# A prologue in another order: second keys projected early into other PSUM banks, loads from two queues, two roundings moved

## The chip, the cores and the metric

One core of a Trainium2 chip runs one transformer block, everything in one launch. The metric is the device time in microseconds. The kernel is written engine by engine: TensorE (PE), VectorE (DVE), ScalarE (ACT), GpSimd (POOL) and SyncE (SP) each have one list of instructions, and semaphores tie the lists together. An engine never passes over an instruction that waits, so the order of each list matters.

## The reference

The input `x` is 4 batches of 256 rows of 256 numbers, and `ctx_2048` has the same shape. Cut to what matters:

```
h  = layernorm(x);  hq = fp8_round(h / in_scale) * in_scale      # for q, qx, k, v: four roundings
q, qx = hq @ wq.T, hq @ wqx.T          # 16 heads of 128 each
k, v  = hq @ wk.T, hq @ wv.T           # 8 groups of 128
kx,vx = split(ctx @ w_kv_x.T)          # 8 groups, from the context, not rounded
each of q, qx, k, kx: layernorm over its 128 numbers
self  = softmax(q k') v;  cross = softmax(qx kx') vx             # grouped-query attention
x1 = x + tanh(g_xattn) * fp8_round([self, cross] * smooth) @ wproj.T
x2 = x1 + tanh(g_ffn) * (routed top-6 of 64 experts + shared expert)(layernorm(x1))
```

The change touches only the start: the first layernorm, its roundings, and the first keys and values.

## The kernel before, in words

**The loop.** After a prologue, all engines run the same written-out loop `for i in range(NSUB + MAXLAG)`, 34 rounds. A round starts one sub-block `s0 = sub(i)` (two of the 16 heads, for both kinds of attention, for one batch) and carries on the two before it, `s1` and `s2`. `n = a // 2` names a unit (one batch and one pair of groups), `t` one half (128 rows) of its sequence. `kv_at(i)` says which half of which unit's keys and values a round projects: round 0 does (0, 1), round 1 does (1, 0), round 2 does (1, 1), and so on. Half (0, 0) is done in the prologue. After the loop come the router and the experts.

**The prologue, per engine.** SP loads x for batches 0 and 1, seven of fifteen small vectors (`load_vectors`, L388), x for batches 2 and 3, the first key and value weights (`load_kv(0, 0)`, L409), the context (L436), the cross-attention weights (`load_kv(0, 1)`) and the first query weights. ACT issues the other eight vectors and then eight scalars `scal` (L700), before its first computation. All vectors land in rows of one tile, `vec_rows`, which PE turns once all fifteen are there (L1431); DVE takes them over (`vectors`, L971).

For each batch b of x: DVE takes statistics (`ln_stats`), POOL raises to the power -1/2 (`ln_rstd`), DVE normalises (`ln_norm`), PE turns the result (`transpose_h`), ACT scales it (`ln_out(b)`, L651) and writes four scaled copies (`quant_y(b)`, L660), and then DVE rounds them to fp8 by adding and taking away a magic number: `quant_exponents(b)` and `quant_round(b)`. The last subtraction is POOL's for batches 0 and 1 (`quant_sub`, L509) and DVE's for 2 and 3 (`quant_less`, L1001). Only two batches have buffers (`q_y[b % 2]`, `q_mg[b % 2]`), and these lie over tiles that the loop needs: `q_mg[0]` over `qk_f`, so the first turned keys (`evac_Tk(0, 0)`, L764) wait for three roundings (`xq_ready` 3). Before, the fourth batch's rounding stands on DVE in round 0, ahead of the sums of the first queries' squares.

PE also turns the context (`transpose_ctx`, through the two banks of `pT_ps`, which the loop later uses for turned probabilities) and the weights (`fill_kv`, `fill_wq`, through the two banks `aux_ps`); for each, ACT takes the high part (`ctx_hi`, `kv_hi`, `wq_hi`) and DVE the rest (`ctx_lo`, `kv_lo`, `wq_lo`), each matrix being kept as a high and a low float.

**Keys.** `project_kv(n, t)` (L1449) writes both kinds of keys and values of one half into the two banks of `proj_ps`. ACT squares the keys (`squares_kv`, L728) and copies the values out (`evac_v`, L742); DVE sums (`sums`, L1079); POOL makes the reciprocal root (`rstd_of`, L519); DVE scales (`scaled_kv`, L1085, signals `qk_normed`). The queries' `project_q`, `squares_q`, `rstd_q` and `scaled_q` do the same, in the same two banks `proj_ps`, so each projection waits for the scaling of the one before it (`wait(pe, qk_normed, seq)`). The scaled tiles are turned by PE (`fill_Tk`, `fill_Tq`), taken out by ACT (`evac_Tk`, `k_hi`, `evac_Tq`, `q_hi`) and finished by DVE (`qk_lo`, L1108); then `scores` can start (L1520).

Of the kernel before, what the change touches and what calls it, by code (L numbers as in the profile page):

```python
# [5 lines left out]
def flamingo_kernel(nc: bass.Bass, t: dict, out: bass.AP):  # L6
# [38 lines left out]
    with ctx:  # L45
# [346 lines left out]

        @block.sync
        def _(sp):
# [11 lines left out]
            def load_rows(dst, name, row, n, done):  # L406
                sp.dma_start(dst, t[name][row:row + n * D, :].rearrange("(r p) h -> p r h", p=P)).then_inc(done, 16)

            def load_kv(j, x):  # L409

                a, b = ((("L0_xattn_wk", 0), ("L0_xattn_wv", 0)), (("L0_xattn_w_kv_x", 0), ("L0_xattn_w_kv_x", G * D)))[x]
                load_rows(w_raw[:, 4 * x:4 * x + 2, :], a[0], a[1] + 2 * j * D, 2, w_loaded[x])
                load_rows(w_raw[:, 4 * x + 2:4 * x + 4, :], b[0], b[1] + 2 * j * D, 2, w_loaded[x])

            def load_wq(g, dst, done):

                load_rows(dst[:, 0:2, :], "L0_xattn_wq", g * HPG * D, 2, done)
                load_rows(dst[:, 2:4, :], "L0_xattn_wqx", g * HPG * D, 2, done)
# [22 lines left out]
            load_kv(1, 0)  # L441
# [5 lines left out]
            for j in range(G // 2):  # L447
                if j > 0:
# [4 lines left out]
                    if j + 1 < G // 2:  # L453
                        sp.wait_ge(aux_filled, Fill("WQ", 1, 2 * j).filled)
                        load_kv(j + 1, 0)
                sp.wait_ge(aux_filled, Fill("WQ", 1, 2 * j + 1).filled)
                if j + 1 < G // 2:
                    load_kv(j + 1, 1)
# [33 lines left out]
        def _(pool):  # L492
# [26 lines left out]
            def rstd_of(seq, last, w):  # L519

                at = slice(0, 4) if w == 4 else slice(4, 12)
# [9 lines left out]
            def rstd_kv(n, t):  # L531

                rstd_of(kv_seq(n, t), kv_seq(n - 1 + t, 1 - t) if (n, t) != (0, 0) else -1, 4)

            def rstd_q(s):
                rstd_of(q_seq(s.a), q_seq(s.a - 1) if s.a else -1, 8)
# [26 lines left out]
            rstd_kv(0, 0)  # L563
            quant_sub(1)
            for i in range(NSUB + MAXLAG):
# [5 lines left out]
                if kv:  # L571
                    rstd_kv(*kv)
# [70 lines left out]
        def _(act):  # L643
# [53 lines left out]
            act.wait_ge(rows_clear, 1)  # L697
            load_vectors(act, VECTORS[7:])
# [6 lines left out]
            ln_out(1)  # L705
            quant_y(1)
# [7 lines left out]
            ln_out(2)  # L714
            quant_y(2)
# [12 lines left out]
            def squares_kv(n, t):  # L728
# [3 lines left out]
                nc.scalar.activation(sq[:, 0:4 * D].rearrange("p (a b) -> p a b", a=2), proj_ps[:, :, 0:2 * D],  # L732
# [9 lines left out]
            def evac_v(n, t):  # L742
# [3 lines left out]
                if at >= VRING:  # L746
                    act.wait_ge(aux_filled, Fill("Vx", 2 * ((at - VRING) // 2) + 1).filled)
                nc.scalar.activation(v_sb[:, at % VRING, :, :, :].rearrange("p y g d -> p y (g d)"),
                                     proj_ps[:, :, 2 * D:4 * D], ACT.Copy).then_inc(v_ready, 1)
# [83 lines left out]
            evac_v(0, 0)  # L833
            wq_hi(0, 0)
            wq_hi(1, 0)
            ln_out(3)
            for i in range(NSUB + MAXLAG):
# [4 lines left out]
                if kv:  # L842
                    squares_kv(*kv)
# [3 lines left out]
                if kv:  # L847
                    evac_v(*kv)
                if i == 0:
                    quant_y(3)  # L850
# [88 lines left out]
        def _(dve):  # L939
# [139 lines left out]
            def sums(seq, w):  # L1079

                dve.wait_ge(sq_ready, seq + 1)
                nc.vector.tensor_reduce(ss[:, w - 4:2 * w - 4], sq[:, 0:w * D].rearrange("p (a d) -> p a d", d=D), AX.X,  # L1082
                                        ALU.add).then_inc(ss_ready, 1)

            def scaled_kv(n, t):  # L1085
# [3 lines left out]
                if n > 0:  # L1089
# [3 lines left out]
                    proj_ps[:, :, 0:2 * D].rearrange("p x (a d) -> p x a d", d=D),  # L1093
                    rstd[:, 0:4].rearrange("p (x a) -> p x a", x=2).unsqueeze(3).to_broadcast([P, 2, 2, D]),
# [124 lines left out]
            quant_exponents(2)  # L1219
            scaled_kv(0, 0)  # L1220
            wq_lo(0, 0)
            wq_lo(1, 0)
            quant_round(2)
            for i in range(NSUB + MAXLAG):
                s0, s1, s2, kv = sub(i), sub(i - 1), sub(i - 2), kv_at(i)
                if kv:
                    sums(kv_seq(*kv), 4)
# [9 lines left out]
                if kv:  # L1237
# [143 lines left out]
        def _(pe):  # L1381
# [67 lines left out]
            def project_kv(n, t):  # L1449
# [20 lines left out]
                for i, (c, a, w) in enumerate(terms):  # L1470
                    ins = nc.tensor.matmul(proj_ps[:, 1, :], ctxT[:, a, c, tok], wkvT[:, w, c, 1, :],  # L1471
# [3 lines left out]
            def project_q(s):  # L1475
# [4 lines left out]
                wait(pe, qk_normed, seq)  # L1480
                wait(pe, v_ready, min(s.a + 2, 2 * NU))
# [332 lines left out]
```

## Time and profile before

| | us |
|---|---|
| median of 3 runs (lowest to highest) | 804.56 (802.93 to 805.38) |
| the profiled execution, its own time | 801.96 |
| its span, first to last instruction | 800.1 |

| engine | busy us | share of the span |
|---|---|---|
| PE | 718.0 | 90% |
| DVE | 604.1 | 76% |
| ACT | 466.1 | 58% |
| POOL | 447.4 | 56% |

The busy time says how long an engine worked, the span how long the whole took. The mean granted clock of PE was 0.977 of full speed. The profile has several views: the page with its slices, the timeline of an engine (each row: start, duration, what, and in brackets the idle time before it and who ended it), the chain of waits, the windows. The part that the change touches lies in the first 60 us.

### The profile page before, as it was taken

How to read it: one execution, taken by the hardware profiler on the slowest of the kernel's cores; microseconds unless marked ns; L12 is line 12 of the kernel's file. 1: busy time of each engine (PE TensorE's matmuls, PEld its weight loads, DVE VectorE, ACT ScalarE, POOL GpSimd, SP SyncE). 2: the span in 40 equal slices, each digit the busy share in tenths (PEclk: the TensorE clock that was granted, in tenths of full speed). 3: DMA queues.
4: the chain of work that ended last, by engine and by line, in shares of the span. 5: the costliest groups of instructions: out<-in, count | busy, mean ns of one | idle time of the engine just before them, and what ended most of it. 6: DMA issues, size and time to landing. Idle time of an engine off the chain costs nothing.

```text
span 800.1 us, 15318 instructions
## 1 busy us (share of the span) xinstructions
PE 718.0 (90%) x4857; PEld 582.8 (73%) x4857; DVE 604.1 (76%) x1286; ACT 466.1 (58%) x1179; POOL 447.4 (56%) x586
## 2 busy tenths in 40 slices
PE   3648899899999989999998999998978778999996
PEld 3546787788788778878877887887756556777775
DVE  6867888788888878888887888889888673444444
ACT  5646767677676767767666776866754322222221
POOL 3415777566777756677775667776766223222220
PEclk9979999999999999999999999999999897999999
DMA  5310100100010010001001010000010104666661
GB/s 185 112 53 1 53 3 1 54 28 28 0 45 10 1 54 27 27 1 40 16 1 54 1 34 2 27 1 2 1 42 19 67 9 132 195 190 189 192 186 54
DMA packets 44478, 42.74 MB, mean 53 GB/s; under 512 B 3717, under 2 KB 43386, under 8 KB 44410
## 3 DMA queue, kind: packets, MB, share of 16 engines
q1 hardware_dynamic: 41706, 36.61, 14.9%
q0 software_dynamic: 1536, 5.28, 2.5%
q8 instruction: 35, 0.57, 0.3%
q14 instruction: 33, 0.27, 0.1%
q10 hardware_dynamic: 1168, 0.01, 0.1%
HBM read 39.52 MB, written 2.37 MB: 52 GB/s over the span
## 4 chain that ended last, share of the span: by engine, by line
PE 63%; DVE 18%; ACT 6%; issue 6%; POOL 4%; DMA 1%; SPq 1%; POOLq 0%; DVEq 0%; ACTq 0%
PE out_ps L1748 9%; PE s_ps L1530 6%; PE proj_ps L1486 6%; PE proj_ps L1471 6%; PE pT_ps L1539 5%; DVE q_tok L1102 5%; PE aux_ps L1549 4%; PE aux_ps L1500 4%; PE aux_ps L1563 4%; PE proj_ps L1462 4%; PE work_ps L1740 3%; POOL rstd L528 3%; DVE pT_sb L1127 3%; DVE ss L1082 3%; PE work_ps L1762 2%
## 5 line engine op out<-in xcount | busy, mean ns | idle before, releaser
L543 POOL TENSOR_SCALAR p_sb<-p_sb,psum_row 128x256 f32<-128x256 f32 x256 | 125.0, 503 | 67.9 <-DVE psum_row L1121 66.6
L797 ACT ACTIVATE p_sb<-s_ps,negmax 128x256 f32<-128x256 f32 x256 | 118.3, 473 | 64.1 <-DVE negmax L1116 63.0
L1549 PE MATMUL aux_ps<-pT_sb,v_sb 128*128 128x512 f32 x256 | 120.7, 594 | 4.0 <-DVE pT_sb L1127 4.0
L1530 PE MATMUL s_ps<-kT,qT 128*128 128x256 f32 x768 | 112.3, 289 | 8.2 <-DVE qT L1112 4.6
L1127 DVE COPY pT_sb<-pT_ps 128x512 f32<-128x512 f32 x128 | 87.7, 686 | 41.3 <-PE pT_ps L1539 40.8
L550 POOL TENSOR_TENSOR y_bf<-y_bf,mg_bf 128x512 bf16<-128x512 bf16 x64 | 85.8, 1341 | 58.5 <-DVE mg_bf L1139 58.5
L1530 PEld LDWEIGHTS s_ps<-kT,qT 128*128 128x128 f32 x768 | 97.6, 190 | 18.3 <-issue 18.3
L1116 DVE TENSOR_REDUCE negmax<-s_ps 128x2 f32<-128x512 f32 x128 | 86.5, 683 | 5.9 <-PE s_ps L1530 5.6
L528 POOL TENSOR_TENSOR rstd<-var,minus_half 128x8 f32<-128x8 f32 (+1 forms) x64 | 85.7, 1339 | 5.3
L553 POOL TENSOR_TENSOR catq<-y_bf,mg_bf 128x512 fp32r<-128x512 bf16 x64 | 79.5, 1243 | 5.0
L1748 PE MATMUL out_ps<-eo,onehot 128*128 128x256 f32 x512 | 74.2, 297 | 0.6 <-ACT eo L909 0.6
L1563 PE MATMUL aux_ps<-wpT,catq 128*128 128x256 f32 x512 | 69.2, 288 | 5.9 <-DVE wkvT L1030 4.8
L1748 PEld LDWEIGHTS out_ps<-eo,onehot 128*128 128x128 f32 x512 | 66.2, 193 | 9.9 <-issue 8.6
L1539 PE MATMUL pT_ps<-ident,p_sb 128*128 128x128 f32 x512 | 72.0, 273 | 0.9 <-POOL p_sb L543 0.7
L633 POOL DMA_INDIRECT gx<-rows_dram,idx_cur x32 | 33.0, 1031 | 69.0 <-DVE w_slot L1331 59.8
L1486 PE MATMUL proj_ps<-wqT,xq 128*128 128x256 f32 x512 | 67.0, 284 | 4.0 <-DVE k_tok L1091 4.0
L1549 PEld LDWEIGHTS aux_ps<-pT_sb,v_sb 128*128 128x128 f32 x256 | 44.1, 190 | 35.4 <-issue 35.4
L1563 PEld LDWEIGHTS aux_ps<-wpT,catq 128*128 128x128 f32 x512 | 63.2, 191 | 6.8 <-DVE wkvT L1030 5.5
L1486 PEld LDWEIGHTS proj_ps<-wqT,xq 128*128 128x128 f32 x512 | 63.6, 191 | 4.3 <-issue 4.3
L1539 PEld LDWEIGHTS pT_ps<-ident,p_sb 128*128 128x128 f32 x512 | 59.4, 140 | 6.6 <-POOL p_sb L543 2.5
L760 ACT ACTIVATE qk_f<-aux_ps,vec 128x512 f32<-128x512 f32 x64 | 49.8, 778 | 23.6 <-PE aux_ps L1500 21.0
L909 ACT ACTIVATE eo<-work_ps,w_slot 128x256 fp32r<-128x256 f32 x32 | 15.2, 474 | 82.7 <-PE work_ps L1762 82.7
(181 smaller groups left out, 1399.2 us busy)
## 6 DMA issues: line engine op xcount, KB each, us to landing
w_up_a<-in_L_ffn_gate_up_proj SPq DMA_DIRECT2D x16, 384.0 KB, 3.5
w_up_b<-in_L_ffn_gate_up_proj SPq DMA_DIRECT2D x16, 384.0 KB, 3.6
wp_raw<-in_L_xattn_wproj SPq DMA_DIRECT2D x16, 256.0 KB, 2.9
w_down_a<-in_L_ffn_down_proj SPq DMA_DIRECT2D x16, 192.0 KB, 3.5
w_down_b<-in_L_ffn_down_proj SPq DMA_DIRECT2D x16, 192.0 KB, 3.6
w_raw<-in_L_xattn_w_kv_x SPq DMA_DIRECT2D x8, 256.0 KB, 3.3
w_raw<-in_L_xattn_wq SPq DMA_DIRECT2D x7, 256.0 KB, 2.7
w_raw<-in_L_xattn_wqx SPq DMA_DIRECT2D x7, 256.0 KB, 2.9
```

The lines of the kernel that those rows point to most:

```text
L528: nc.gpsimd.tensor_tensor(rstd[:, at], var8[:, at], minus_half[:, 0:w], ALU.pow).then_inc(rstd_ready, 1)
L543: ins = nc.gpsimd.tensor_scalar(p_sb[:, r, st, :], p_sb[:, r, st, :], rsum[:, r, st:st + 1], 1.0, ALU.mult, ALU.mult)
L550: nc.gpsimd.tensor_tensor(yc_bf[:, ty, :], yc_bf[:, ty, :], mg_bf[:, ty, :], ALU.add).then_inc(catq_ready, 1)
L797: ins = nc.scalar.activation(p_sb[:, r, st, :], s_ps[:, r % 2, st, :], ACT.Exp, bias=negmax[:, r, st:st + 1], accum_out=psum_row[:, r, st: ...
L1116: nc.vector.tensor_reduce(negmax[:, r, :], s_ps[:, r % 2, :, :], AX.X, ALU.max, negate=True).then_inc(max_ready, 1)
L1127: nc.vector.tensor_copy(pT_sb[:, r // 2, r % 2, :, :], pT_ps[:, r % 2, :, :]).then_inc(pT_ready, 1)
L1486: ins = nc.tensor.matmul(proj_ps[:, t, x * 256:(x + 1) * 256], xq[:, s.b, 3 * x, c, t * P:(t + 1) * P], wqT[:, s.gi, part, c, x * 256:(x + ...
L1530: ins = nc.tensor.matmul(s_ps[:, k % 2, st, :], qT[:, a, ty, h, st * P:(st + 1) * P], kT[:, b, ty, s.gi, :], start=(i == 0), stop=(i == 2))
L1539: ins = nc.tensor.transpose(pT_ps[:, r % 2, tt, st * P:(st + 1) * P], p_sb[:, r, st, tt * P:(tt + 1) * P], ident[:, :])
L1549: ins = nc.tensor.matmul(aux_ps[:, f.bank, :], v_sb[:, (2 * s.n + tt) % VRING, ty, s.gi, :], pT_sb[:, ty, :, tt, :], start=(tt == 0), stop ...
L1563: ins = nc.tensor.matmul(aux_ps[:, f.bank, tt * H:(tt + 1) * H], catq[:, s.gi, blk, tt * P:(tt + 1) * P], wpT[:, s.gi, part, blk, :], star ...
L1748: ins = nc.tensor.matmul(out_ps[:, n, :], onehot[:, u % 2, n * P:(n + 1) * P], eo[:, part, :], start=False, stop=False, skip_group_check=True)
```

## The change

All of `x` is issued first on SP, then all fifteen vectors, then the first query weights. ACT issues the first key and value weights, the context and the cross-attention weights, then the scalars. The second half of the first unit's keys, (0, 1), leaves round 0: it is projected straight behind (0, 0), into the banks of `pT_ps`, and has its own four places in `ss`, `var8` and `rstd` (`kv_stats`). ACT does `ln_out(1)`, `quant_y(1)` behind the weights and context instead of before them, and batch 2 behind both halves of the keys and the first query weights. The fourth batch's rounding moves on DVE behind `qk_lo` of the first turned keys, and on ACT behind `k_hi`.

```diff
+        def kv_ps(n, t):
+            return pT_ps[:, :, :, :].rearrange("p a b c -> p a (b c)") if (n, t) == (0, 1) else proj_ps[:, :, :]
+
+        def kv_stats(n, t):
+            return slice(4, 8) if (n, t) == (0, 1) else slice(0, 4)
...
 @block.sync
-            load_x(0)
-            load_x(1)
+            for b in range(NB):
+                load_x(b)
             sp.wait_ge(rows_clear, 1)
-            load_vectors(sp, VECTORS[:7])
-            load_x(2)
-            load_x(3)
+            load_vectors(sp, VECTORS)
...
-            load_kv(0, 0)
-            sp.dma_start(ctx_raw, t["ctx_2048"].rearrange("b (n p) h -> p (b n) h", p=P)).then_inc(ctx_loaded, 16)
-            load_kv(0, 1)
             load_wq(0, wq0_raw, wq0_loaded)
...
 @block.gpsimd
-                rstd_of(kv_seq(n, t), kv_seq(n - 1 + t, 1 - t) if (n, t) != (0, 0) else -1, 4)
+                rstd_of(kv_seq(n, t), kv_seq(n - 1 + t, 1 - t) if n > 0 else -1, kv_stats(n, t), 4)
...
             rstd_kv(0, 0)
+            rstd_kv(0, 1)
             quant_sub(1)
...
 @block.scalar
-            act.wait_ge(rows_clear, 1)
-            load_vectors(act, VECTORS[7:])
+            load_kv(act, 0, 0)
+            act.dma_start(ctx_raw, t["ctx_2048"].rearrange("b (n p) h -> p (b n) h", p=P)).then_inc(ctx_loaded, 16)
+            load_kv(act, 0, 1)
...
             ln_out(0)
             quant_y(0)
-            ln_out(1)
-            quant_y(1)
             ctx_hi(0)
             ctx_hi(1)
...
             ctx_hi(2)
             ctx_hi(3)
-            ln_out(2)
-            quant_y(2)
+            ln_out(1)
+            quant_y(1)
...
             squares_kv(0, 0)
             evac_v(0, 0)
+            squares_kv(0, 1)
+            evac_v(0, 1)
             wq_hi(0, 0)
             wq_hi(1, 0)
+            ln_out(2)
+            quant_y(2)
             ln_out(3)
             for i in range(NSUB + MAXLAG):
...
-                if kv:
+                if kv and i > 0:
                     squares_kv(*kv)
...
-                if i == 0:
-                    quant_y(3)
...
                     k_hi(s0.n, 0)
+                if i == 0:
+                    quant_y(3)
...
 @block.vector
             quant_exponents(1)
             quant_round(1)
             sums(0, 4)
-            quant_exponents(2)
+            sums(kv_seq(0, 1), 4)
             scaled_kv(0, 0)
+            scaled_kv(0, 1)
             wq_lo(0, 0)
             wq_lo(1, 0)
+            quant_exponents(2)
             quant_round(2)
...
-                if i == 0:
-                    quant_exponents(3)
-                    quant_round(3)
-                    quant_less(3)
                 if s0:
                     sums(q_seq(s0.a), 8)
...
                     qk_lo(s0.n, "TKs")
+                if i == 0:
+                    quant_exponents(3)
+                    quant_round(3)
+                    quant_less(3)
...
 @block.tensor
-                wait(pe, qk_normed, seq)
-                wait(pe, v_ready, 2 * n + t)
+                if (n, t) == (0, 1):
+                    pe.wait_ge(ctx_ready, 4)
+                else:
+                    wait(pe, qk_normed, seq)
+                    wait(pe, v_ready, 2 * n + t)
...
-                wait(pe, qk_normed, seq)
-                wait(pe, v_ready, min(s.a + 2, 2 * NU))
+                wait(pe, qk_normed, seq if s.a else 1)
+                wait(pe, v_ready, min(s.a + 2, 2 * NU) if s.a else 1)
...
             project_kv(0, 0)
+            project_kv(0, 1)
             fill_wq(0, 0)
             fill_wq(1, 0)
```

PE's own list of the prologue is otherwise as it was: `transpose_h(3)`, the last thing ahead of `project_kv(0, 0)`, waits for `ln_out(1)` (`yT_ready` 2).

## Rows read from the trace of the kernel before

**Rows 1.** The page: busy time by engine.

```profile
PE 718.0 (90%) x4857; PEld 582.8 (73%) x4857; DVE 604.1 (76%) x1286; ACT 466.1 (58%) x1179; POOL 447.4 (56%) x586
```

**Rows 2.** The chain of waits, 0 to 60 us: start, duration, what.

```profile
6.11 8.63 DMA p_sb<-in_ctx
...
25.53 3.31 ACT wp_raw L666 x8
...
47.64 2.29 DVE xq L1005
...
51.54 1.65 POOL rstd L528
```

**Rows 3.** Timeline of the queue on SP.

```profile
0.75 0.97 SPq L396 DMA_DIRECT2D x_sb<-in_x  x2
1.77 0.36 SPq L391 DMA_DIRECT2D sq<-in_L_xattn_ln_w  x1
...
3.73 0.32 SPq L391 DMA_DIRECT2D sq<-in_L_xattn_proj_smooth  x1
...
6.69 3.07 SPq L407 DMA_DIRECT2D w_raw<-in_L_xattn_w_kv_x  x2
```

**Rows 4.** Timeline of ACT.

```profile
7.22 0.58 ACTq L700 DMA_DIRECT2D scal<-in_g_ffn  x1
7.83 1.28 ACT L702 ACT_TABLE_LOAD   x1 [7.83 <-issue]
...
9.23 1.00 ACT L656 ACTIVATE acc<-s_ps,vec 128x256 f32<-128x256 f32 x2
...
23.51 1.08 ACT L647 ACTIVATE ctxT<-pT_ps 128x512 fp32r<-128x512 f32 x2
...
28.74 0.58 ACT L732 ACTIVATE sq<-proj_ps 128x512 f32<-128x512 f32 x1
...
31.12 1.03 ACT L656 ACTIVATE acc<-s_ps,vec 128x256 f32<-128x256 f32 x2
```

**Rows 5.** Timeline of DVE.

```profile
7.24 0.21 DVE L974 COPY vec<-proj_ps 128x52 f32<-128x52 f32 x1 [0.74 <-PE proj_ps L1431]
...
13.42 0.62 DVE L983 TENSOR_SCALAR wscale<-vec,scal 128x2 f32<-128x2 f32 x4 [0.43 <-DMA scal<-in_g_ffn]
...
19.86 0.88 DVE L1027 SCALAR_TENSOR_TENSOR wkvT<-aux_ps,wscale,wkvT 128x256 fp32r<-128x256 f32 x2 [0.84 <-ACT wkvT L680]
...
34.50 2.33 DVE L998 TENSOR_SCALAR qk_f<-qk_f 128x2048 bf16<-128x2048 bf16 x1
...
44.21 0.68 DVE L992 TENSOR_SCALAR v_sb<-v_sb 128x2048 bf16<-128x2048 bf16 x1
...
49.85 1.21 DVE L1082 TENSOR_REDUCE ss<-sq 128x8 f32<-128x1024 f32 x1
53.21 1.23 DVE L1102 TENSOR_TENSOR q_tok<-proj_ps,rstd 128x1024 f32<-128x1024 f32 x1 [2.15 <-POOL rstd L528]
...
57.18 0.69 DVE L1112 TENSOR_TENSOR qT<-qk_f,qT 128x512 fp32r<-128x512 f32 x1 [2.15 <-ACT qT L782]
```

**Rows 6.** Timeline of PE.

```profile
6.75 0.45 PE L1431 MATMUL proj_ps<-ident,sq 128*128 128x128 f32 x1 [6.75 <-DMA sq<-in_L_xattn_proj_smooth]
...
17.40 1.06 PE L1407 MATMUL aux_ps<-center,w_raw 128*128 128x128 f32 x4
...
22.08 0.68 PE L1407 MATMUL aux_ps<-center,w_raw 128*128 128x128 f32 x4 [0.30 <-DVE wkvT L1027]
...
33.12 1.61 PE L1462 MATMUL proj_ps<-wkvT,xq 128*128 128x256 f32 x8 [4.08 <-DVE k_tok L1091]
...
59.52 1.67 PE L1530 MATMUL s_ps<-kT,qT 128*128 128x256 f32 x12
```

**Rows 7.** Timeline of POOL.

```profile
32.21 4.07 POOL L512 TENSOR_TENSOR xq<-v_sb,y_bf 128x2048 fp32r<-128x2048 bf16 x1
```

**Rows 8.** DMA issues of 0 to 40 us: KB each, median us from issue to landing.

```profile
scal<-in_g_ffn ACTq DMA_DIRECT2D x1, 0.5 KB, 6.2
```

More of the change, by code:

```diff
@@ L391, in load_vectors, with load_rows, load_kv @@
                 eng.dma_start(vec_rows[row:row + n, :], t[name].rearrange("(r p) -> r p", p=P)).then_inc(vec_loaded, 16)
+        def load_rows(eng, dst, name, row, n, done):
+            eng.dma_start(dst, t[name][row:row + n * D, :].rearrange("(r p) h -> p r h", p=P)).then_inc(done, 16)
+        def load_kv(eng, j, x):
+            a, b = ((("L0_xattn_wk", 0), ("L0_xattn_wv", 0)), (("L0_xattn_w_kv_x", 0), ("L0_xattn_w_kv_x", G * D)))[x]
+            load_rows(eng, w_raw[:, 4 * x:4 * x + 2, :], a[0], a[1] + 2 * j * D, 2, w_loaded[x])
+            load_rows(eng, w_raw[:, 4 * x + 2:4 * x + 4, :], b[0], b[1] + 2 * j * D, 2, w_loaded[x])
         @block.sync
@@ L397, in load_x @@
                              ).then_inc(x_loaded[b], 16)
-            load_x(0)
-            load_x(1)
+            for b in range(NB):
+                load_x(b)
             sp.wait_ge(rows_clear, 1)
-            load_vectors(sp, VECTORS[:7])
-            load_x(2)
-            load_x(3)
[L406 to L413, printed above, removed]
+            load_vectors(sp, VECTORS)
             def load_wq(g, dst, done):
-                load_rows(dst[:, 0:2, :], "L0_xattn_wq", g * HPG * D, 2, done)
-                load_rows(dst[:, 2:4, :], "L0_xattn_wqx", g * HPG * D, 2, done)
+                load_rows(sp, dst[:, 0:2, :], "L0_xattn_wq", g * HPG * D, 2, done)
+                load_rows(sp, dst[:, 2:4, :], "L0_xattn_wqx", g * HPG * D, 2, done)
             def load_wp(g):
@@ L440, in _ @@
             load_wq(1, w_raw[:, 4:8, :], w_loaded[1])
-            load_kv(1, 0)
+            load_kv(sp, 1, 0)
             sp.wait_ge(aux_filled, Fill("WQ", 1, 0).filled)
@@ L454, in _ @@
                         sp.wait_ge(aux_filled, Fill("WQ", 1, 2 * j).filled)
-                        load_kv(j + 1, 0)
+                        load_kv(sp, j + 1, 0)
                 sp.wait_ge(aux_filled, Fill("WQ", 1, 2 * j + 1).filled)
                 if j + 1 < G // 2:
-                    load_kv(j + 1, 1)
+                    load_kv(sp, j + 1, 1)
                 else:
@@ L517, in _, with rstd_of @@
             quant_sub(0)
-            def rstd_of(seq, last, w):
-                at = slice(0, 4) if w == 4 else slice(4, 12)
+            def rstd_of(seq, last, at, w):
                 pool.wait_ge(ss_ready, seq + 1)
@@ L731, in squares_kv @@
                 wait(act, ss_ready, seq)
-                nc.scalar.activation(sq[:, 0:4 * D].rearrange("p (a b) -> p a b", a=2), proj_ps[:, :, 0:2 * D],
+                nc.scalar.activation(sq[:, 0:4 * D].rearrange("p (a b) -> p a b", a=2), kv_ps(n, t)[:, :, 0:2 * D],
                                      ACT.Square).then_inc(sq_ready, 1)
@@ L748, in evac_v @@
                 nc.scalar.activation(v_sb[:, at % VRING, :, :, :].rearrange("p y g d -> p y (g d)"),
-                                     proj_ps[:, :, 2 * D:4 * D], ACT.Copy).then_inc(v_ready, 1)
+                                     kv_ps(n, t)[:, :, 2 * D:4 * D], ACT.Copy).then_inc(v_ready, 1)
             def evac_Tq(s, ty):
@@ L841, in _ @@
                     k_hi(s1.n, 1)
-                if kv:
+                if kv and i > 0:
                     squares_kv(*kv)
@@ L846, in _ @@
                 weights_hi(i, 1)
-                if kv:
+                if kv and i > 0:
                     evac_v(*kv)
-                if i == 0:
-                    quant_y(3)
                 if i == 2:
@@ L1225, in _ @@
                 s0, s1, s2, kv = sub(i), sub(i - 1), sub(i - 2), kv_at(i)
-                if kv:
+                if kv and i > 0:
                     sums(kv_seq(*kv), 4)
@@ L1236, in _ @@
                     recip(s1, 0)
-                if kv:
+                if kv and i > 0:
                     scaled_kv(*kv)
@@ L1461, in project_kv @@
                         for part in range(2):
-                            nc.tensor.matmul(proj_ps[:, 0, ty * 256:(ty + 1) * 256],
+                            nc.tensor.matmul(kv_ps(n, t)[:, 0, ty * 256:(ty + 1) * 256],
                                              xq[:, b, 1 + ty, c, t * P:(t + 1) * P],
@@ L1470, in project_kv @@
                 for i, (c, a, w) in enumerate(terms):
-                    ins = nc.tensor.matmul(proj_ps[:, 1, :], ctxT[:, a, c, tok], wkvT[:, w, c, 1, :],
+                    ins = nc.tensor.matmul(kv_ps(n, t)[:, 1, :], ctxT[:, a, c, tok], wkvT[:, w, c, 1, :],
                                            start=(i == 0), stop=(i == len(terms) - 1))
@@ L1617, in _ @@
                 s0, s1, s2, kv = sub(i), sub(i - 1), sub(i - 2), kv_at(i)
-                if kv:
+                if kv and i > 0:
                     project_kv(*kv)
```

9 lines of the change are left out of this document (5 added, 4 removed).

## The prediction

> **What bounds the kernel now, and how I read it.** The page first: PE is busy for 90% of the span [rows 1], and nearly all of that is the loop and the experts, which the change leaves alone. So the question is by how much the start of the steady loop moves, and that is settled in the first 60 us, where PE mostly waits. The chain of waits there [rows 2] shows what ends last: the landing of the context at 14.74 us (6.11 + 8.63), then ACT's scaled copies of batch 2 (3.31), the rounding of batch 3 on DVE (the last of it 2.29), POOL's root (1.65). It passes through four engines, so I read their timelines next, each for two marks. Mark S is where ACT starts `ctx_hi(2)`, 23.51 us: by then the first weights are converted. Mark F is the first score matmul, 59.52 us, after which both kernels run the same instructions [rows 4, 6]. Before, F - S = 36.0 us. The change moves S by its loads and its early order, and F - S by its late order. I work out both.
>
> **Loads.** The SP queue issued two of x in 0.97 us (the next row starts 1.02 after it) and seven vectors in 2.28 us, 1.77 to 4.05, so 0.33 each; ACT issued eight more of the same kind beside them [rows 3]. Now SP issues four of x and all fifteen vectors: 0.75 + 2.04 + 15 x 0.33 = 7.7 us for the end of the last, at the 0.30 of the shortest 7.3. From the start of the last issue of before (3.73) to PE's first instruction (6.75) were 3.02 us [rows 3, 6]. Thus the vectors are all there at about 7.2 + 3.0 = 10.2 us, against 6.75: 3.5 us later. Bounds: 9.2 if the last one, a single row now and not the 16 KB of `proj_smooth`, lands 1 us faster after its issue (my guess; the least that its place allows is 6.75 plus eight issues of 0.30 more, the same 9.2); 12.0 if it is slowed as `scal` was (6.2 us from issue to landing, beside 1 KB packets of the big loads [rows 8]), in part. I take 10.3, near to the row of the same kind of load.
>
> The context is issued at about 2.0 us instead of 6.11. It needed 8.6 us and then released PE [rows 2]. With x on the other queue sharing the same engines I expect 10 to 12 us, and PE wants it only after the vectors and two turns of x, at about 13: hidden, as are the weights. So the wait that the chain shows, for the context, goes, and the vectors are late in its place. A rule of the Trainium skill speaks on this: "DMA: Bandwidth & Descriptors", section "Issuing engines are not separate DMA queues", says that transfers started by different engines run on the same 16 DMA engines and that a second issuer saves only issue time. By it the second queue gives no bandwidth, and the loads' total, 3.5 MB, ends no sooner; I expect the same, and the sum doesn't rest on it.
>
> **From the vectors to S.** PE's turn ends and DVE starts `vectors` 0.49 us after PE starts (6.75 to 7.24) [rows 5, 6]: 10.3 + 0.05 + 0.5 = 10.85. Behind that instruction on DVE stand, as before, the normalising of batch 1 and the statistics and normalising of 2 and 3, and then `weight_scales`, which started at 13.42 [rows 5], after 6.18 us with waits of about 1.0 for data in them (0.30 and 0.43 were for DMAs). So `weight_scales` ends 10.85 + 5.1 + 0.5 = 16.45. On ACT: `ln_out(0)` stood at 9.23, released by the end of the table load (7.83 + 1.28 = 9.11) [rows 4], and now stands at 11.75, released by the vectors; the copies come 4.35 us later (1.0 + 3.3), at 16.1. Both meet. The first rounding (44.21 to 47.64 for its like [rows 2, 5]: 3.4 us) ends at 19.85, `ctx_lo(0)` adds 0.6, and `kv_lo` of the first weights starts at 20.5 against 19.86 [rows 5]: +0.64. What is gained there is that ACT no longer does batch 1 first (4.3 us); what eats it is the 3.5 us of the vectors less the 1.1 that the table load had covered, and DVE, which stands behind them.
>
> PE now idles about 4 us before the third weight fill, as it waits for `kv_lo`. After idling, its four matmuls of a fill took 1.06 us, later 0.68 [rows 6]. Two fills and the context turns at the slower pace cost 0.55, 0.55 and 0.4, of which ACT's steps between hide some: I take +0.9 (bounds 0 and 1.5). S = 23.51 + 0.64 + 0.9 = 25.05: **+1.5 us**.
>
> **From S to F.** In the new order, all from rows: two `ctx_hi` 0.95 and `ln_out(1)` 1.05 and the copies of batch 1 3.31 [rows 2, 4] give 5.3. DVE rounds batch 1, 3.43, to 8.75; before, this had been done under ACT's copies of batch 2, and now `sums(0)` stands behind it. `project_kv(0, 0)`, PE's turn of batch 3, which waits for `ln_out(1)`, and `project_kv(0, 1)` lie under these 8.75: the first eight matmuls of such a projection took 1.61 us even after idling (33.12) [rows 6]. Without that cover each would come onto the chain whole. `sums(0)` is half of the 1.21, so 0.7: 9.5. It releases ACT's `squares_kv(0, 1)` (one tile `sq`), and squares, values and four halves of `wq_hi` took 2.38 (28.74 to 31.12) [rows 4]: 11.9. Batch 2 on ACT 1.05 + 3.31: 16.3. Its rounding 3.43 and `quant_less(2)` 2.29: 22.0. Two `wq_lo`, each like `kv_lo` 0.8: 23.6. The queries' sums 1.2, the root until `scaled_q` 3.36 - 1.2 = 2.15 (49.85 to 53.21), `scaled_q` 1.15 [rows 5]: 28.1. `qk_lo` of the keys 0.7: 28.8. Now the fourth rounding, 49.85 - 44.21 = 5.64 [rows 5]: 34.45. `qk_lo` of the queries 0.7: 35.2, and the scores can start. So F - S is **35.2 against 36.0, -0.8 us**.
>
> Why so little for a moved 5.6 us: before, a wait of 2.15 us stood in front of the queries' `qk_lo` at 57.18, while PE turned and ACT copied [rows 5]. The rounding fills that wait, and the other 3.5 us come onto the chain in its new place. The wait for the second keys' root, with which POOL stood behind `quant_less`, is what the early projection saves, and it is paid with the rounding of batch 1, now bare. PE's projections cost the same in number. Of `project_q` nothing is late: it needs `wq_lo` of the first weights, at about 14 us after S, and its squares wait for DVE.
>
> One collision goes: a DVE rounding step of 0.7 took 2.33 us (34.50) beside POOL's 4.07 of `quant_sub(1)` (32.21) [rows 5, 7]. In the new order POOL's subtraction runs while DVE does `wq_lo`. The Trainium skill, "SBUF — State Buffer", has a rule that GpSimd and a fast-mode DVE instruction lock each other out for the whole instruction. The trace agrees in the 2.33. My sum has every rounding at 3.43, so this is in it; if they met again it would be 1.6 us more.
>
> **The sum.** +1.5 - 0.8 = +0.7. The queue of ACT (below) may bind a little: I take +0.9 for the likeliest. Against the profiled execution (span 800.1, its own time 801.96) this is 802.9; the median of the runs is 2.6 above that execution, so **805.5 us**. After F nothing stands out that would give it back or multiply it. About 0.3%, 2.4 us, is what a measurement of this kernel can tell from no change.
>
> **Rivals.**
> (a) The loads help after all: the vectors land at 9.2 and PE keeps its pace. S is then 23.51 - 1.1 + 0.64 = 23.05, F moves by -0.5 - 0.8 = -1.3: 803.3. For it: the landing of 3.0 had x beside it. Against: more is in flight now.
> (b) Slower: ACT's own queue holds ACT. Before, two cross-attention loads behind the context took 3.07 us to issue instead of 1.0 [rows 3]. Now ACT issues these, and behind them eight scalars, which took 0.6 each near the end, and the table load. 1.0 + 1.6 + 3.1 + 8 x 0.6 = 10.5, and if the scalars wait for room as well, at 1 us each, 13.7; with the table load 15.0 for `ln_out(0)`, and the last scalar, 6.2 us from issue to landing [rows 8], at 19 for `weight_scales`, which stands in front of the first rounding. It decides from 11.75 for ACT or 16 for the scalars; it would cost 15.0 - 11.75 = 3.3 us, with my 0.7 +4.0: 808.6. For it: the scalars lie behind 2 MB in one queue. Against: at their issue, half of that has not yet met the backlog under which the 3.07 was seen.
> (c) Faster: the old order carried small losses that my rows see as durations and which go, and the loads help too. Were the root of the queries' sums 0.6 shorter, the two `wq_lo` done under `quant_less(2)`'s waits, and (a) true, it were -1.3 - 0.6 - 0.8 = -2.7: 801.9. Against: `wq_lo` stands behind `quant_less(2)` in DVE's list.
> (d) The banks: the second keys' projection doesn't run beside the first's scaling, since `ctx_lo(3)` frees them late. It changes nothing, since PE is idle there: as forecast.
>
> **How the numbers follow.** Forecast with (d) 0.42, from 804.3 to 807; (a) 0.20; (b) 0.26; (c) 0.12. The first two are within 0.3%: 0.62 same. (b) is slower, 0.26; (c) faster, 0.12. The range to hold 8 in 10: from 802.3, between (c) and (a), to 808.8, the end of (b) without its tail.
>
> **What would show it.** In the changed profile: PE's first instruction at 10.3 (9.2 for (a), over 12 for (b)); the first `ln_out` behind the vectors, not behind ACT's queue; `ctx_hi(2)` at 25.0; DVE's first sums behind the rounding of batch 1, at S + 8.8; the queries' `qk_lo` straight behind the fourth subtraction, with no wait; the first score at 60.3 or so. I am wrong in the load part if ACT's table load ends after 12 or `weight_scales` waits for a scalar past 17; in the order part if F - S is outside 34 to 36.5; and in the whole if F moves by one number and the end by another, over 1 us apart.

## The result, and the profile after

The changed kernel takes 805.8 us in the median of 15 runs (802.99 to 807.67), the kernel before 803.01 beside it (801.85 to 805.38): ratio 1.0024, 95% interval 1.0013 to 1.0035, so 1.9 us or a quarter of a per cent slower (the two medians lie 2.8 us apart). The forecast was +0.9 us and 805.5 us, no change within 0.3%. The profiled execution took 805.06 us with a span of 803.3; the engines' busy times are those of before within 2.4 us (PE 717.9, DVE 602.3, ACT 466.2, POOL 445.0), so the change moved waits and no work.

The chain of waits of the changed kernel, 0 to 62 us (start, duration, what), answers to [rows 2]:

```profile
7.16 4.09 DMA sq<-in_L_xattn_kxln_b
...
28.26 3.32 ACT v_sb L667 x8
...
33.78 1.23 DVE v_sb L1003
...
45.96 2.29 DVE xq L1009
48.26 1.57 DVE wqT L1045 x4
```

The context (8.6 us) is gone from it. In its place stands the landing of the last of the fifteen vectors, and behind it DVE's roundings of batches 1 and 2.

The timelines after, first SP's queue and ACT, against [rows 3, 4]:

```profile
0.75 2.00 SPq L411 DMA_DIRECT2D x_sb<-in_x  x4
...
7.16 0.25 SPq L397 DMA_DIRECT2D sq<-in_L_xattn_kxln_b  x1
```

```profile
2.33 1.50 ACTq L400 DMA_DIRECT2D w_raw<-in_L_xattn_w_kv_x  x2
3.86 1.03 ACTq L702 DMA_DIRECT2D scal<-in_L_xattn_wq_scale  x1
...
9.08 1.28 ACT L704 ACT_TABLE_LOAD   x1 [9.08 <-issue]
...
12.79 1.02 ACT L657 ACTIVATE acc<-s_ps,vec 128x256 f32<-128x256 f32 x2 [2.22 <-DVE rvec L981]
...
25.88 0.60 ACT L648 ACTIVATE ctxT<-pT_ps 128x512 fp32r<-128x512 f32 x1 [0.26 <-PE pT_ps L1405]
```

Then PE and DVE, against [rows 5, 6]:

```profile
11.39 0.44 PE L1438 MATMUL proj_ps<-ident,sq 128*128 128x128 f32 x1 [11.39 <-DMA sq<-in_L_xattn_kxln_b]
...
23.50 1.06 PE L1414 MATMUL aux_ps<-center,w_raw 128*128 128x128 f32 x4
...
61.27 1.66 PE L1540 MATMUL s_ps<-kT,qT 128*128 128x256 f32 x12 [1.69 <-issue]
```

```profile
21.57 1.65 DVE L1031 SCALAR_TENSOR_TENSOR wkvT<-aux_ps,wscale,wkvT 128x256 fp32r<-128x256 f32 x4
...
34.93 0.68 DVE L1087 TENSOR_REDUCE ss<-sq 128x4 f32<-128x512 f32 x1
...
49.74 1.21 DVE L1087 TENSOR_REDUCE ss<-sq 128x8 f32<-128x1024 f32 x1
...
60.49 0.68 DVE L1117 TENSOR_TENSOR qT<-qk_f,qT 128x512 fp32r<-128x512 f32 x1
```

| mark | before, first trace | before, second (e9) | forecast | after, first | after, second (e10) |
|---|---|---|---|---|---|
| vectors, PE's first instruction | 6.75 | 6.60 | 10.3 | 11.39 | 11.88 |
| `ln_out(0)` | 9.23 | 10.34 | 11.75 | 12.79 | 13.28 |
| first `kv_lo` | 19.86 | 20.62 | 20.5 | 21.57 | 22.06 |
| S, `ctx_hi(2)` | 23.51 | 24.29 | 25.05 | 25.88 | 26.51 |
| F, first score | 59.52 | 60.64 | 60.3 | 61.27 | 61.56 |
| F - S | 36.0 | 36.35 | 35.2 | 35.4 | 35.05 |
| second `scaled_q` of the loop | 70.25 | 71.37 | | 71.78 | 72.09 |
| last `scaled_q` of the loop | 594.7 | 597.2 | | 597.8 | 598.1 |

The loop starts 0.4 to 1.8 us later by these four traces, and the last rows show a second difference, which is no part of the prologue. In the first pair the distance is 1.53 us at the second `scaled_q` and 1.61 at one near 542 us, and then 3.1. The windows of that place, before and after (window, sum, busy time of the engines, granted clock, DMA):

```profile
552.00:556.00 4.00, 2.88 (x24) 2.91 (x25) 3.26 (x9) 2.52 (x10) 2.86 (x6) 1.00 0.01 2
```

```profile
553.50:557.50 4.00, 2.77 (x16) 2.81 (x17) 3.26 (x9) 2.62 (x10) 2.86 (x6) 0.76 0.01 2
```

and the two queries' projections there, the kernel before first:

```profile
553.91 2.05 PE L1486 MATMUL proj_ps<-wqT,xq 128*128 128x256 f32 x16
```

```profile
555.52 3.54 PE L1496 MATMUL proj_ps<-wqT,xq 128*128 128x256 f32 x16
```

In both kernels PE waited 2.4 us for DVE ahead of the score just before this place. In one trace the granted clock stayed at 2.4 GHz; in the other it fell for a while to 1.2 (0.76 in the window's mean), and the sixteen matmuls took 1.5 us longer. All fourteen traces of this case have that wait of 2.4 us. From 552 to 564 us the mean granted clock is 0.86 in seven of them and 1.00 in the other seven, and where it is 0.86 the next `scaled_q` comes 1.4 to 1.5 us later.

### The profile page after: what moved, and what is told of

It reads as the page before. It is cut to its first block, busy times and chain, and to the rows that moved or that the text cites. A ratio compares the mean times of both kernels' runs of the same rounds, so it can differ in the third digit from the quotient of the medians.

```text
span 803.3 us, 15318 instructions
## 1 busy us (share of the span) xinstructions
PE 717.9 (89%) x4857; PEld 583.4 (73%) x4857; DVE 602.3 (75%) x1286; ACT 466.2 (58%) x1179; POOL 445.0 (55%) x586
## 4 chain that ended last, share of the span: by engine, by line
PE 62%; DVE 20%; ACT 6%; issue 6%; POOL 4%; DMA 1%; SPq 1%; POOLq 0%; DVEq 0%; ACTq 0%
PE out_ps L1759 9%; PE proj_ps L1496 6%; PE s_ps L1540 6%; PE pT_ps L1549 5%; PE proj_ps L1481 5%; DVE q_tok L1107 5%; PE aux_ps L1559 4%; PE aux_ps L1573 4%; PE aux_ps L1510 4%; PE proj_ps L1472 3%; PE work_ps L1751 3%; POOL rstd L528 3%; DVE ss L1087 3%; PE work_ps L1773 2%; DVE pT_sb L1132 2%
## 5 line engine op out<-in xcount | busy, mean ns | idle before, releaser
L797 ACT ACTIVATE p_sb<-s_ps,negmax 128x256 f32<-128x256 f32 x256 | 118.2, 472 | 64.1 <-DVE negmax L1121 63.0
L1559 PEld LDWEIGHTS aux_ps<-pT_sb,v_sb 128*128 128x128 f32 x256 | 44.0, 190 | 35.4 <-issue 35.4
L1549 PEld LDWEIGHTS pT_ps<-ident,p_sb 128*128 128x128 f32 x512 | 59.5, 141 | 6.6 <-POOL p_sb L543 2.5
L1087 DVE TENSOR_REDUCE ss<-sq 128x8 f32<-128x1024 f32 (+1 forms) x64 | 60.4, 944 | 0.7 <-ACT sq L732 0.7
```

Source lines behind the costliest of these rows:

```text
L797: ins = nc.scalar.activation(p_sb[:, r, st, :], s_ps[:, r % 2, st, :], ACT.Exp, bias=negmax[:, r, st:st + 1], accum_out=psum_row[:, r, st: ...
L1549: ins = nc.tensor.transpose(pT_ps[:, r % 2, tt, st * P:(st + 1) * P], p_sb[:, r, st, tt * P:(tt + 1) * P], ident[:, :])
L1559: ins = nc.tensor.matmul(aux_ps[:, f.bank, :], v_sb[:, (2 * s.n + tt) % VRING, ty, s.gi, :], pT_sb[:, ty, :, tt, :], start=(tt == 0), stop ...
```

## The experiments

Marks are times in us of one profiled execution each; ratios are against the kernel before on the same chip, with 95% intervals.

**e1: old loads.** The order of after with the loads of before.

```diff
-            for b in range(NB):
-                load_x(b)
+            load_x(0)
+            load_x(1)
             sp.wait_ge(rows_clear, 1)
-            load_vectors(sp, VECTORS)
+            load_vectors(sp, VECTORS[:7])
+            load_x(2)
+            load_x(3)
...
+            load_kv(sp, 0, 0)
+            sp.dma_start(ctx_raw, ...).then_inc(ctx_loaded, 16)
+            load_kv(sp, 0, 1)
             load_wq(0, wq0_raw, wq0_loaded)
...
-            load_kv(act, 0, 0)
-            act.dma_start(ctx_raw, ...).then_inc(ctx_loaded, 16)
-            load_kv(act, 0, 1)
+            act.wait_ge(rows_clear, 1)
+            load_vectors(act, VECTORS[7:])
```

> The changed kernel with the loads of the kernel before (all big loads from SP, seven vectors on SP and eight on ACT); the new order of the work is kept. Theory (late vectors): the vectors reach PE at 6.8 us instead of 11.4, and S (ctx_hi(2)) goes from 25.9 back to about 23.4, now held by the landing of the context at 14.7; F - S stays 35.4, so F = 58.8, 0.7 below the kernel before's 59.5, and the time is 802.3 beside 803.0. Rival (the order itself costs time, the loads are nearly free): S stays over 25 and F over 60.5.

Measured: vectors 6.57, S 23.46, F 58.70, F - S 35.2; 801.1 us against 804.2, ratio 0.997 (0.996 to 0.9981). The new loads are the loss, and what they make late on the chain is the vectors. Without them the new order alone is a gain: 2.4 us by the timed runs, 0.8 by F against the first trace of before and 1.9 against e9's.

**e2: loads alone.** The order of before with the loads of after (the reverse of the diff above, on the kernel before).

> The kernel before with the new loads alone (all x and all vectors on SP, weights and context on ACT), its order of work kept. Theory (late vectors): ln_out(0) at 12.8 instead of 9.2, so everything behind it is 3.6 us late: S 27.1, F 63.1 to 64, time 806.6 to 807.5. Rival (the loads' part is harmless, since the context lands earlier): F within 1 us of 59.5.

Measured: vectors 11.95, S 28.48, F 65.46; 808.55 us, ratio 1.0062 (1.0044 to 1.008), +5.0 us. The direction is that of late vectors, the size above the theory's (F 63.1 to 64): F is 5.9 later than in the first trace of before, 4.8 than in the second. `ln_out(0)` stands at 13.35, and ACT does batch 1 straight behind it, so the first `kv_lo` comes at 23.67, 3.8 us later than in the first trace of before and 3.1 than in the second. The rest up to S is PE's: its third and fourth weight fill took 1.19 and 1.06 us for four matmuls, where they took 0.68 before.

In the new order the same loads cost 61.27 - 58.70 = 2.6 us of F (2.9 with the second trace of after). By F, then, the new order hides about half of what the new loads cost. The timed runs don't show this: e1 and e2 add up to -2.4 + 5.0 = +2.6 us, and the whole change measured +1.9 and, in e10, +2.2, which is the same within the intervals (0.9 to 1.4 us either way).

**e3: the fourth rounding back.**

```diff
+                if i == 0:
+                    quant_exponents(3)
+                    quant_round(3)
+                    quant_less(3)
                 if s0:
                     sums(q_seq(s0.a), 8)
...
                     qk_lo(s0.n, "TKs")
-                if i == 0:
-                    quant_exponents(3)
-                    quant_round(3)
-                    quant_less(3)
```

(and `quant_y(3)` on ACT back behind `evac_v`.)

> The changed kernel with the fourth batch's rounding back in its old place on DVE and ACT, ahead of the sums of the first queries' squares. Theory (the move behind the turned keys fills a wait of about 2 us): F is 1.6 to 2.1 us later than 61.3, so 62.9 to 63.4. Rival (the move costs, since it stands between the turned keys and queries): F is earlier than 61.3.

Measured: S 26.95, F 65.93, F - S 39.0 against 35.4; ratio 1.0077 (1.006 to 1.0094). The move is worth 3.6 us, not 2. The timeline of DVE and of PE in e3:

```profile
63.43 0.69 DVE L1117 TENSOR_TENSOR qT<-qk_f,qT 128x512 fp32r<-128x512 f32 x1 [2.15 <-ACT qT L782]
```

```profile
62.36 1.97 PE L1472 MATMUL proj_ps<-wkvT,xq 128*128 128x256 f32 x8
64.17 1.56 PE L1481 MATMUL proj_ps<-wkvT,ctxT 128*128 128x512 f32 x6
65.57 0.60 PE L1510 MATMUL aux_ps<-ident,q_tok 128*128 128x128 f32 x4
65.93 1.68 PE L1540 MATMUL s_ps<-kT,qT 128*128 128x256 f32 x12
```

The 2.15 us wait is back, as expected, but the queries are complete at 64.1 and the score starts at 65.93: PE's next key projection, started at 62.36, stands in front. In the new place the rounding covers this projection too. I had counted one cover and there are two. The ratios give 4.3 us, with the vectors 0.8 us later in e3's trace.

**e7: the second keys back** in round 0 and in `proj_ps`, all else as changed (undoes `kv_ps`, `kv_stats` and the moved calls of `project_kv`, `squares_kv`, `evac_v`, `sums`, `rstd_kv`, `scaled_kv`).

```diff
             project_kv(0, 0)
-            project_kv(0, 1)
...
-                if kv and i > 0:
+                if kv:
                     project_kv(*kv)
...
-                wait(pe, qk_normed, seq if s.a else 1)
+                wait(pe, qk_normed, seq)
```

> The changed kernel with the second half of the first keys back in round 0 and in the banks of proj_ps; loads and all roundings as changed. Theory (the early projection takes a projection, POOL's root and a collision off the chain): the first queries' projection waits for the second keys' scaling again, and F is about 2.5 us later than 61.3, 63.8. Rival (the early projection gives nothing, as it puts its squares ahead of batch 2 on ACT): F within 0.5 of 61.3 or earlier.

Measured: S 25.41, F 65.28, F - S 39.9; ratio 1.0082 (1.0065 to 1.0098). The early projection is worth 4.5 us of F - S, more than the 2.5. Its PE and DVE timelines:

```profile
48.89 3.76 PE L1488 MATMUL proj_ps<-wqT,xq 128*128 128x256 f32 x16 [5.51 <-DVE k_tok L1093]
```

```profile
39.21 2.03 DVE L993 TENSOR_SCALAR wp_raw<-wp_raw 128x2048 bf16<-128x2048 bf16 x1 [0.27 <-ACT wp_raw L666]
...
53.74 1.22 DVE L1084 TENSOR_REDUCE ss<-sq 128x8 f32<-128x1024 f32 x1 [4.32 <-ACT sq L738]
```

The queries' projection waits for the second keys' scaling; after that wait it takes 3.76 us, against 2.15 in the changed kernel (started at 43.55), and the queries' sums wait 4.3 us. The rounding of batch 2 meets POOL (2.03 instead of 0.69).

The F - S of e3 (39.0) and of e7 (39.9) are both above the 36.0 of before, because a third move stays in both: ACT's batch 1 (4.3 us) stands behind S and no longer ahead of it. That move was never run by itself, so what it is worth isn't shown.

**e4: vectors first,** then weights and context from ACT as changed.

```diff
+            act.wait_ge(rows_clear, 1)
+            load_vectors(act, VECTORS[7:])
             load_kv(act, 0, 0)
             act.dma_start(ctx_raw, ...).then_inc(ctx_loaded, 16)
             load_kv(act, 0, 1)
```

(SP's list as in e1 up to the fourth x.)

> The changed kernel with the vectors split and issued as before (seven on SP behind two loads of x, eight first on ACT), but weights and context still on ACT behind them. Theory (late vectors, and ACT held by what it issues): the vectors are there at 6.8, but ACT is busy with issues (1.0 + 2.6 for vectors, 3.0 for five loads, 5.0 for the scalars) until 11.6 and with the table load until 12.9, so ln_out(0) is at 13 as in the changed kernel and S and F hardly move: F 61 to 61.8. Rival (only the vectors matter): ln_out(0) near 10, F 59 or earlier.

Measured: vectors 6.55, S 26.27, F 61.89; ratio 1.0019 (1.0005 to 1.0033). ACT in e4:

```profile
7.63 1.16 ACTq L706 DMA_DIRECT2D scal<-in_L_xattn_wv_scale  x1
...
11.77 1.28 ACT L708 ACT_TABLE_LOAD   x1 [11.77 <-issue]
...
13.17 1.00 ACT L659 ACTIVATE acc<-s_ps,vec 128x256 f32<-128x256 f32 x2
```

This is rival (b) of the forecast, once the vectors no longer cover it: ACT issues 21 transfers and loads its table before it computes. The new loads lose either way, by late vectors or by a late ACT. F is 0.1 us beyond the theory's 61 to 61.8.

**e5: early sums.** In the changed kernel `sums(0)` stands behind the whole rounding of batch 1, and releases ACT's second squares.

```diff
             quant_exponents(1)
-            quant_round(1)
             sums(0, 4)
+            quant_round(1)
             sums(kv_seq(0, 1), 4)
```

> The changed kernel with DVE's sums(0) between quant_exponents(1) and quant_round(1) instead of behind both. Theory (the first sums stand late on the chain and release ACT's second squares): squares_kv(0, 1) start at 33.8 instead of 35.7, batch 2 is ready 1.9 us earlier, but its rounding then meets POOL's quant_sub(1) and is held, so that F is 0.8 earlier, 60.5. Rival A (no lock between POOL and DVE): F 1.9 earlier, 59.4. Rival B (the chain doesn't run through the sums): F stays 61.3.

Measured: F - S 34.7 against 35.4; F 61.35, since the vectors came at 12.18 in this run, 0.8 later than in the first trace of after. Ratio 1.0003 (0.9991 to 1.0015). By F - S the gain is 0.7, near the 0.8; the ratios differ by 1.7 us, of which a part may be the clock behind 540 us (1.00 in this trace, 0.86 in both traces of after). DVE and POOL:

```profile
41.42 1.67 DVE L996 TENSOR_SCALAR wp_raw<-wp_raw 128x2048 bf16<-128x2048 bf16 x1 [0.63 <-ACT wp_raw L667]
```

```profile
38.47 4.07 POOL L513 TENSOR_TENSOR xq<-v_sb,y_bf 128x2048 fp32r<-128x2048 bf16 x1
```

The rounding step ends 0.55 us behind POOL's subtraction and takes 1.67 instead of 0.69: the lock that the forecast spoke of, met again by coming earlier.

**e6: the fourth rounding later,** behind both `qk_lo`.

```diff
                 if s0 and s0.gi == 0:
                     qk_lo(s0.n, "TKx")
+                if i == 0:
+                    quant_exponents(3)
+                    quant_round(3)
+                    quant_less(3)
```

(taken from behind `qk_lo` of `TKs`.)

> The changed kernel with DVE's fourth rounding behind the qk_lo of both the queries and the second turned keys. Theory: F comes 1.7 us earlier, at 59.6, where PE ends its projection, but the 5.6 us then stand in front of the first maxima, which start at about 65 instead of 62.3, so the steady loop is 2.4 us later than in the changed kernel. Rival (the first score is what counts): the loop is 1.7 earlier.

Measured: F 59.43, first maxima 65.36, as expected, but the second `scaled_q` at 76.29, 4.5 us later than in the changed kernel and not 2.4; ratio 1.0064 (1.0048 to 1.0081). The first score is 1.8 us earlier and the kernel 3.2 us slower than the changed one by the ratios: F was a good mark only as long as the instructions behind it stayed as they were. The maxima are 3.1 us later, and the rest up to 4.5 is the clock. PE in e6, and then at the same place of the changed kernel:

```profile
67.34 1.62 PE L1540 MATMUL s_ps<-kT,qT 128*128 128x256 f32 x6 [6.24 <-DVE qT L1117]
68.76 3.05 PE L1496 MATMUL proj_ps<-wqT,xq 128*128 128x256 f32 x16
```

```profile
64.36 0.95 PE L1540 MATMUL s_ps<-kT,qT 128*128 128x256 f32 x6 [1.43 <-DVE qT L1117]
65.17 2.13 PE L1496 MATMUL proj_ps<-wqT,xq 128*128 128x256 f32 x16
```

The scores start 3.0 us later, behind 6.24 us in which PE was idle, and the granted clock is 0.59 in the mean from 66 to 72 us, against 1.00 from 64 to 68 in the changed kernel. The scores then take 0.7 us longer and the projection 0.9.

**e8: e1 and e5 together.**

> The changed kernel with both the old loads and the early sums(0). Theory: the two gains add, F = 58.8 - 0.8 = 58.0, 1.5 us below the kernel before; time 801.5 beside 803.0. Rival (both work on the same slack): F not below 58.8.

Measured: vectors 6.71, S 24.06, F 58.23, F - S 34.2; 801.38 us against 804.09, ratio 0.9959 (0.9946 to 0.9972), 3.3 us faster than the kernel before and the lowest ratio of all that ran. F is where the theory put it (58.0), and F - S is 1.1 below e1's; F itself is 0.5 below. The interval overlaps that of e1 (0.996 to 0.9981), so that the early sums add to the old loads is shown by the traces and not by the timed runs.

**e9 and e10: both kernels once more,** unchanged.

> The kernel before, unchanged, profiled and timed once more. Theory (the 1.5 us that the changed kernel's trace lost behind F, in the stretch at 555 us where the granted clock fell to 0.76, come by chance in both kernels): F is 59.5 again within 0.5, the ratio is 1 within its interval, and this trace may show such a fall in the stretch behind 540 us, with a span of 801.6 then and 800.1 otherwise. Rival (the fall belongs to the changed kernel's shift): no such fall here, in no run.

> The changed kernel, profiled and timed once more. Theory (chance): S - first matmul and F - S within 0.5 of 14.5 and 35.4; the fall of the clock behind 540 us may be there or not, and where it is missing the span is 801.8. Rival: the fall is at the same round and costs 1.5 us again.

Measured: before again, ratio 0.9999 (0.9987 to 1.0011), F 60.64 and not 59.5, span 801.6. After again, ratio 1.0028 (1.0017 to 1.0039), span 803.2, S less first matmul 14.6. F is 1.1 us later, outside the theory's 0.5, and 0.8 of it is there at S. The first trace of before was a lucky one in the prologue. ACT there and in e9:

```profile
7.22 0.58 ACTq L700 DMA_DIRECT2D scal<-in_g_ffn  x1
```

```profile
7.35 1.55 ACTq L700 DMA_DIRECT2D scal<-in_g_ffn  x1
8.93 1.28 ACT L702 ACT_TABLE_LOAD   x1 [8.93 <-issue]
```

The last issue took 1.55 us instead of 0.58, and `ln_out(0)` came at 10.34. In e1 and e8, which have the same loads, that issue took 1.40 and 1.53 us and `ln_out(0)` came at 10.23 and 10.32. And the slow projection is there in both second traces, e9 first:

```profile
555.61 2.85 PE L1486 MATMUL proj_ps<-wqT,xq 128*128 128x256 f32 x16
```

```profile
556.29 3.01 PE L1496 MATMUL proj_ps<-wqT,xq 128*128 128x256 f32 x16
```

So the fall came in the changed kernel at the same round again, as e10's rival has it, but also in the kernel before, as e9's theory has it.

**e11: four scalars late.** On e8: the four scalars that the first weights don't need are issued behind the last `kv_hi`.

```diff
+            load_scalars(0, 4)
...
             for c, x in KV_ORDER:
                 kv_hi(c, x, 0)
+            load_scalars(4, 8)
             ctx_hi(2)
```

> The combined kernel (old loads, early sums) with only the four scalars that the weights need issued ahead of ACT's first work, and the other four behind the last kv_hi. Theory (S is held by the context's landing and the weight fills behind it on PE): ln_out(0) comes at 8.1 instead of 10.3 and weight_scales at 13.9 instead of 14.7, but the first kv_lo stays at 20.3 to 20.5 and F at 58.0 to 58.3. Rival (ACT's queue holds S): S and F 0.8 to 2 us earlier.

**e12: fills first.** On e11, PE's first two `fill_kv` ahead of `transpose_ctx(0)`.

```diff
+            for c, x in KV_ORDER[:2]:
+                fill_kv(c, x, 0)
             for i in range(2):
                 transpose_ctx(i)
             transpose_h(2)
-            for c, x in KV_ORDER:
+            for c, x in KV_ORDER[2:]:
                 fill_kv(c, x, 0)
```

> As e11, and on PE the two first weight fills ahead of the first two context turns, so that they run while the context is under way. Theory (the fills behind the context hold S): the first kv_lo starts at 18.5 instead of 20.5, S at 22.2, F at 56.4, and the time is 799.6 beside 803.0 to 804. Rival (DVE, with the rounding of batch 0, or the landing of the cross-attention weights at 16.5 holds it): F not below 57.7.

Measured: e11 has `ln_out(0)` at 7.96 and the first `kv_lo` at 20.54, as the theory says, but S at 25.7 and F at 60.6; ratio 0.9989 (0.9978 to 1.0001). e12 has `kv_lo` at 18.87 (1.7 earlier), S 24.21, F 58.9; ratio 0.9975 (0.9965 to 0.9985). Neither beats e8 (S 24.06, F 58.23). e11's F is neither the theory's 58.0 to 58.3 nor the rival's, and e12's is on the rival's side of 57.7, far from the theory's 56.4. ACT in e11:

```profile
23.72 0.60 ACT L689 ACTIVATE wkvT<-aux_ps 128x512 fp32r<-128x512 f32 x1 [0.62 <-PE aux_ps L1424]
...
25.17 0.48 ACTq L707 DMA_DIRECT2D scal<-in_g_ffn  x1
25.70 1.09 ACT L653 ACTIVATE ctxT<-pT_ps 128x512 fp32r<-128x512 f32 x2 [1.38 <-issue]
```

My edit put four issues of 0.5 us between `kv_hi` and `ctx_hi(2)`, on the chain. The earlier start of ACT brought nothing there, since the first `kv_lo` is at 20.54 in e8 as well, and the issues put S 1.6 us later. So e11 shows that ACT's queue doesn't hold `kv_lo` with the old loads, and the Fs of both runs decide nothing else. The gain of the earlier fills is real up to `kv_lo`; what it would be with the issues elsewhere wasn't tried.

## Why the prediction was right, step by step

**The loads: right place, undersized.** The last vector was issued at 7.16, as worked out (7.2), but landed 4.1 us later (the chain's row) and reached PE at 11.39; the seven traces with these loads have it at 11.39, 11.48, 11.52, 11.88, 11.95 and twice 12.18, two of them above my upper bound of 12.0. My 10.3 took the landing of a time when little else was moving (18 GB/s from 4 to 6 us of before). Now, from 3 to 11 us, the windows of after show 371 GB/s for both queues. The term that was mis-sized is the 3.0 from the last issue to PE's first instruction: 4.2 in the first trace of after, 5.0 in e5. Two things hold the vectors up at once, 1 MB of x ahead of them on SP's queue and 2 MB beside them on ACT's, and no run separates the two. The context and the weights were hidden, as said: the first weights' conversion stood behind DVE, and that behind the vectors. I had also expected the loads to end no sooner. They ended at 14.9 us instead of 17.3; the rate while they run is nearly the same (356 GB/s from 11 to 15 us of before), but the lull after 4 us is gone.

**From the vectors to S: right.** First `kv_lo` 10.18 us behind PE's first instruction, forecast 10.2. From there to S 4.3, forecast 4.55 with the 0.9 for PE's slower fills; in the trace the third fill ran at 0.70 for four matmuls, the fourth at the slow 1.06, and the context's last turns took 1.89 for eight (1.04 before). So S moved by 2.4 us and by 2.2 in the second pair, for a forecast of 1.5, and what is missing is the 1.1 of the vectors.

**From S to F: right, 35.4 and 35.05 for 35.2,** with two errors in the reasons behind it. Mark by mark the walk holds: DVE's first sums at S + 9.05 for 8.8, the end of the fourth rounding at S + 34.6 for 34.45. The move of the fourth rounding hides not only the 2.15 us wait but PE's projection (e3: 3.6 in all), and the early second keys are worth 4.5 (e7), not one collision and a root. That the sum is right nevertheless is because it was made by walking the new order down, row by row, and not by adding such worths to the old time.

**The rivals.** (a) is excluded: the vectors weren't at 9.2. Its bound was also too low: I wrote that their place in the list allows 9.2, and left out the two loads of x that now stand ahead of them as well (1.0 us), so it is 10.2. (b), ACT's own queue: issues ended at 9.04, the table load at 10.36, 2.4 us ahead of `ln_out(0)`, and `weight_scales` at 17.13 waited for no scalar; it didn't bind, though it is real, as e4 shows. (c) is excluded with (a). (d) holds in its outcome, that the banks cost nothing, but not in its reason: `ctx_lo(3)` ended at 28.04, ahead of both projections, and PE did the second at 31.17, straight behind the first.

**The whole.** That 805.5 stands so near to the measured 805.8 is luck. It was counted from 804.56, the median of three runs; fifteen runs of the kernel before have 803.01, so the base was 1.5 us too high, and the shift of 0.9 was 1.0 to 1.9 too small. What was right is the mechanism of both steps and that they nearly cancel.

F moved by 1.75 in the first pair of traces, against the forecast's 0.7 to 0.9, and by 0.9 in the second. The span moved by 3.2 in the first pair and 1.6 in the second. In the first pair F and the end are thus 1.45 us apart, which is over the 1 us that I had named as a sign of being wrong in the whole; in the second pair they are 0.7 apart. Two things outside my steps shift the time by as much. The prologue of before varies by 1.1 us at F, 0.8 of it at S with the length of ACT's last issues, so that the rows of one profile gave a base that is better than usual. And behind F a fall of the clock in the last rounds adds 1.4 to 1.5: I had written that nothing stands out there. It is in both traces of after and in one of the two of before, also in e6, e7, e8 and e12, and absent in e1 to e5 and e11, so it isn't tied to the change. The nearest pair are after and e5: both have a `scaled_q` at 543.16 and scores at 554.73 behind 2.40 and 2.41 us of waiting, and the sixteen matmuls took 3.54 and 2.06. So it isn't the shift either.

Whether the change makes the fall likelier stays open, as does what part of the 1.9 us it is. Of 35 timed runs of the kernel before, nine had a mean granted clock of 0.977 or more, as its first trace has, and their median is 802.3; the other 26 have 804.1. None of the 25 of the changed kernel is above 0.976. That points to more falls, but doesn't show them: its own trace with the fall has 0.975, and so has e5's without it.

## What to carry to other kernels

Order the first loads by who waits for them: here a row of 512 bytes that everything needs, issued behind 1 MB on its own queue and beside 2 MB on another, reached PE 4.2 to 5.0 us after its issue, and giving the bulk a queue of its own didn't help it. An engine that both computes and issues transfers pays each issue in its own list (about 0.5 us for a scalar here, up to 1.5), so count them where they stand ahead of its first work (e4) or inside its chain (e11). Take the base of a forecast from many runs and, for the rows, from two traces. To price a reordering, walk the new order down the rows from mark to mark; and take a mark behind which both kernels have the same instructions on every engine.

## What the hardware did that I had not expected

- The last of the vectors reaches PE 3.0 us after its issue with little beside it (`proj_smooth`, 16 KB) and 4.2 to 5.0 behind and beside the bulk (`kxln_b`, 0.5 KB). The issue of one scalar (0.5 KB) took 0.39 to 1.55 us on ACT. The last one of the same list took 0.58 us in one trace and 1.40 to 1.55 in three; why it differs isn't shown.
- A pause of PE that all traces share ends at one clock or at the other from one execution to the next: in the four traces of the two kernels sixteen matmuls took 2.05, 2.85, 3.01 and 3.54 us at the same place of the loop. That alone is a spread of 1.5 us in a kernel of 803.
- In seven traces one step of DVE's rounding started beside POOL's subtraction of 4.1 us. It took between 0.78 and 2.34 us instead of 0.69, and in all seven it ended 0.54 to 0.55 us after POOL did, however early it had started.
